# Order of gathers and scatters in the expert phase, and the length of four tanhs in the opening, of a Mamba and mixture-of-experts kernel

## The reference

```python
xn = layernorm(x)
# first layer, in outline
dA = exp(soft_clamp(dt * A, -8, 8, 0.5))          # soft_clamp is a tanh
def step(h, (dA_t, dB_t, x_t, C_t, t)):
    h = h * dA_t + dB_t * x_t
    fac = min(20 / (norm(h) + 1e-8), 1)           # norm over all of one sequence's state
    h = where(t % 10 == 0, h * fac, h)
    return h, einsum('bdn,bn->bd', h, C_t) + D * x_t
x = x + (xn + scale * (y * silu(gate)) @ W_out.T)
# second layer
gate = softmax(layernorm(x) @ Wg); idx = argmax(gate)
loc = place of the token among those of its expert;  valid = loc < 256
h = relu(einsum('ecm,emf->ecf', dispatched, w1))   # 16 x 256 x 512
expert_out = einsum('ecf,efm->ecm', h, w2)
x = x + (layernorm(x) + expert_out[idx, loc] * (gate[idx] * valid))
```

## Time and profile before

| | us |
|---|---|
| median of 3 runs | 693.81 (693.71 to 693.98) |
| the profiled execution | 692.75 |
| its span, from the first to the last instruction | 690.9 |
| busy: PE | 611.2 (88%) |
| busy: POOL | 581.4 (84%) |
| busy: DVE | 556.6 (81%) |
| busy: ACT | 520.2 (75%) |

### The profile page before, as it was taken

One profiled execution on the slowest core, in us unless ns is written; L12 is line 12 of the kernel. 1 busy time (PEld: TensorE's weight loads), 2 busy tenths in 40 slices (PEclk: granted clock), 3 DMA queues, 4 the chain that ended last, 5 costly groups with the idle time before them and its releaser, 6 DMA issues.

```text
span 690.9 us, 12862 instructions
## 1 busy us (share of the span) xinstructions
PE 611.2 (88%) x4108; PEld 476.0 (69%) x4108; DVE 556.6 (81%) x893; ACT 520.2 (75%) x1012; POOL 581.4 (84%) x413
## 2 busy tenths in 40 slices
PE   8689999999899999989999998999989994599981
PEld 6347677767677677767768677867768783589971
DVE  5658999999999989989999999999989985813320
ACT  3699989999999999999999999999977622112220
POOL 5179999999999999999999999998979972177775
PEclk9989999999999999999999999999999998599996
DMA  4241433236145323724441353325134203446731
GB/s 102 82 153 62 158 111 131 63 118 207 59 150 156 121 68 105 219 72 142 115 148 51 136 176 116 120 73 162 62 121 158 96 1 92 133 144 201 228 106 32
DMA packets 60025, 82.08 MB, mean 119 GB/s; under 512 B 14845, under 2 KB 40738, under 8 KB 59958
## 3 DMA queue, kind: packets, MB, share of 16 engines
q1 hardware_dynamic: 56400, 74.79, 34.1%
q0 software_dynamic: 2608, 6.21, 3.0%
q10 hardware_dynamic: 950, 0.27, 0.2%
HBM read 69.75 MB, written 11.72 MB: 118 GB/s over the span
## 4 chain that ended last, share of the span: by engine, by line
POOL 59%; issue 20%; PE 12%; DVE 3%; DMA 2%; POOLq 1%; ACTq 0%; SPq 0%; ACT 0%; DVEq 0%
POOL h L852 30%; POOL h L866 19%; PE ps L603 3%; PE ps L590 3%; POOL u L839 3%; POOL fac L881 1%; POOL out_dram L399 1%; POOL lnp L813 1%; POOL rstd L888 1%; PE ps L1652 1%; PE ps L610 1%; POOL cq L876 1%; PE ps L570 1%; DMA b0b<-b_d 1%; PE ps L563 1%
## 5 line engine op out<-in xcount | busy, mean ns | idle before, releaser
L1376 DVE TENSOR_TENSOR_SCAN h<-ps,h 128x902 f32<-128x902 f32 x204 | 320.0, 1609 | 21.5 <-ACT ps L993 12.6
L852 POOL TENSOR_TENSOR h<-u,scr 128x1280 f32<-128x1280 f32 x104 | 283.5, 2742 | 2.4
L1768 PEld LDWEIGHTS ps<-h,ident 128*128 128x128 f32 x1632 | 224.7, 190 | 21.8 <-issue 17.3
L1768 PE MATMUL ps<-h,ident 128*128 128x160 f32 x1632 | 231.0, 300 | 1.1 <-issue 0.8
L1102 ACT ACTIVATE z<-dtb,asc 128x240 f32<-128x240 f32 (+3 forms) x432 | 201.5, 536 | 0.1
L993 ACT ACTIVATE ps<-z 128x820 f32<-128x820 f32 (+1 forms) x208 | 137.9, 688 | 21.7 <-DVE h L1376 18.0
L866 POOL TENSOR_TENSOR h<-h,scr 128x1280 f32<-128x1280 f32 (+1 forms) x52 | 138.1, 2656 | 0.7 <-DVE h L1392 0.7
L1427 DVE TENSOR_TENSOR h<-h,ps 128x640 f32<-128x640 f32 (+1 forms) x155 | 87.9, 578 | 0.5 <-issue 0.2
L1652 PE MATMUL ps<-xnT,wT 128*128 128x488 f32 x144 | 72.1, 612 | 0.0
L1003 ACT ACTIVATE sqb<-h 128x208 f32<-128x208 f32 x102 | 45.0, 442 | 26.3 <-DVE h L1376 23.5
L391 POOL DMA_INDIRECT z<-rows_d,gidx x32 | 32.8, 1026 | 32.5 <-DVE gidx L510 23.0
(11 more groups left out here) (203 smaller groups left out, 811.4 us busy)
## 6 DMA issues: line engine op xcount, KB each, us to landing
scr<-b_d SPq DMA_DIRECT2D x52, 640.0 KB, 4.7
scr<-c_d SPq DMA_DIRECT2D x52, 320.0 KB, 4.3
z<-in_L_ffn_w_dram SPq DMA_DIRECT2D x32, 256.0 KB, 3.6
xx_d<-xx SPq DMA_DIRECT2D x8, 256.0 KB, 2.0
xxr<-xx_d SPq DMA_DIRECT2D x8, 256.0 KB, 2.6
rows_d<-h2b SPq DMA_DIRECT2D x16, 120.0 KB, 2.1
rows_d<-xxr SPq DMA_DIRECT2D x16, 120.0 KB, 2.2
out_dram<-xxr SPq DMA_DIRECT2D x16, 120.0 KB, 2.6
```

Of the source, the lines that this page charges most:

```text
L852: pool.tensor_tensor(hr[:, hf * RH:(hf + 1) * RH, 1:SLOT].rearrange("p (n b) t -> p n b t", b=B), us.unsqueeze(1).to_broadcast([P, NST, B, ...
L1376: dve.tensor_tensor_scan(hs, region(G)[:, 0:(r1 - r0) * SLOT], hs, 0.0, ALU.mult, ALU.add).then_inc(gscan, 1)
L1768: pe.matmul(ps[:, YB, 0:H * BS], ident[:], hr[:, :, n * B:(n + 1) * B, 0:SEG], start=(n == 0), stop=False)
```

## The change

Two edits, in POOL's and in ACT's program.

```diff
+        FIRST = 4
...
             pool.wait_ge(idx_ready, 2)
-            for e in range(E):
+            for e in range(AHEAD - 2):
                 pool.wait_ge(fin_made, e + 1)
                 scatter(e)
-                if e + AHEAD < E:
-                    gather(e + AHEAD)
+            for e in range(AHEAD, E):
+                gather(e)
+            for e in range(AHEAD - 2, E):
+                pool.wait_ge(fin_made, e + 1)
+                scatter(e)
...
             def second_half(v, k0, k1):
-                for k in (list(range(NST)) if v == 0 else HALVES)[k0:k1]:
+                for k in (range(max(k0, FIRST), k1) if v == 0 else HALVES[k0:k1]):
                     row_tanh(v, k, HALF * SEG, WIN)
...
-            opening_rows(0, 11, HALF * SEG)
+            opening_rows(0, FIRST, WIN)
+            opening_rows(FIRST, 11, HALF * SEG)
             decay(0)
```

## The result

| | before | changed |
|---|---|---|
| median, us | 693.71 (692.82 to 693.98, 5 runs) | 699.57 (696.78 to 700.38, 5 runs) |
| the profiled execution, us | 692.75 | 700.38 |
| its span, us | 690.9 | 698.6 |
| mean clock granted to PE | 0.965 | 0.955 |

The ratio is 1.0076, with a 95% interval of 1.006 to 1.0093: 0.8% slower, 5.3 us (the medians are 5.9 apart). In a second set of runs it was 1.0082 (1.0069 to 1.0095). The forecast had the sign and +3.5 us, and its range ended at 698.7. The changed kernel spreads over 3.6 us from run to run in this set, the kernel before over 1.2 (over 2.9 and 4.8 in later sets of 23 and 29 runs).

A forecast was written before the change was run, and what follows sets the result against it. The prediction took POOL to bound the expert phase and ACT the opening's first segment. Its terms -0.27 - 0.78 + 3.2 + 1.3 made +3.5 us, a median of 697.3 us, with a range of 695.3 to 698.7.

The forecast's parts named there:

- The bound: POOL ends the expert phase, its 64 indirect DMAs without further gaps; a wait inserted on POOL is paid in full.
- Part 1, the opening: Whole tanhs on ACT: 0.79 us delay swallowed by POOL's 1.10 us idle time, everything behind moves by -0.27 us.
- the second rival: The opening's delay stays: +0.79 us in place of -0.27, 698.4 us; chance 0.12.
- Part 2, fewer changes of kind: Expert phase on POOL: seven fewer changes between gathers and scatters at 0.11 us each, -0.78 us.
- Part 3, the waits on POOL: Expert phase: scatters in a row wait for DVE's results, which come 3.73 us apart; +3.2 us.
- The price of a release: On POOL, a blocked queue pays 0.87 us from release to DMA start; with only 0.30 us, waits would be 2.6.
- Part 4, the stall and its clock: PE idles over 8 us before the ninth expert, then runs at half clock, delaying the last scatters: +1.3 us.
- The first rival: PE doesn't hold up the end; only the waits on POOL are paid: +2.2 us, 696.0 us; chance 0.20.
- The sum: Whole kernel: -0.27 - 0.78 + 3.2 + 1.3 = +3.5 us, median 697.3 us.
- The upper end of the range: 698.7 us, from a long clock return (+0.7) and half of the opening's delay.

The follow-up runs named there:

- eight_scatters: Opening as before; against the changed order on POOL, four experts' scatters between the gathers in place of six: ratio 1.0032 to the kernel before, +2.2 us.
- open_again: The kernel before with only the four whole tanhs of the opening, old order on POOL, second set of runs: ratio 1.0029 to before, +2.0 us.
- both_again: The changed kernel with both edits, run and profiled a second time: 699.25 us, ratio 1.0082 to the kernel before.
- one_by_one: The kernel before with one scatter and one gather by turns in place of two and two: ratio 1.0004, DMA stretch 83.07 us.
- before_again: The unchanged kernel before, run and profiled a second time: 693.96 us, ratio 1.001.
- tail_only: The kernel before with only the new order of gathers and scatters on POOL, opening as before: ratio 1.0062, +4.3 us.

## Why the prediction was wrong, point by point

**The bound** was read rightly. POOL ends the expert phase, and a wait inserted there is paid in full; eight_scatters gave that to 0.03 us.

**Part 1, the opening, had the wrong sign.** ACT's +0.79 and -1.58 us are in the rows (first root +0.61 to +0.83, the scan behind ACT no longer waits while the clock is up). The step that failed is "if the norm comes 0.3 us earlier than before, and its scans have 0.65". The norm needs more than its scans: DVE's queue has the product by the gate of the segment before ahead of it, which waits for PE's sum over the states; PE's queue has that same sum ahead of the norm's; and PE's chain starts with an input that DVE makes right behind the first norm, which is 0.8 us late. In the profile of before this chain and the scans ended together (the scans at 61.73, the product by the gate at 61.65 without a wait), so no idle time pointed at it:

```profile
61.65 0.32 DVE L1361 TENSOR_TENSOR yg<-ps,sgn 128x160 f32<-128x160 f32 x1
```

The second root measured +0.7 and +0.8 us (open_again and both_again, where the clock stayed up) in place of -0.27. This was the second rival, with a chance of 0.12, and what I put against it ("ACT passes its old place at 57.71 earlier") was true and beside the point.

**Part 2, fewer changes of kind, was right in size**: 0.8 us, and the changed kernel's stretch less its waits is 82.08 us, 0.86 below 82.94 (0.9 with all eight gone). As a price of one change that can be multiplied it was wrong: one_by_one has twice the changes and 0.13 us more.

**Part 3, the waits on POOL, is the term that was mis-sized**: +3.2 us, and 4.8 to 5.6 were measured. The step is "the results of the fourth to sixth expert end at 630.41, 634.14 and 637.87". Those were the times of one execution, in which the clock didn't fall during the product of the gates. In ten of the thirteen profiles it falls, and the second to sixth result come 1.6 to 2.5 us later behind the first gather (the second result of both_again 23.2 us behind, of changed and before_again 24.0, in place of 21.55). The kernel before hides this: POOL came to the second scatter 5.0 us after its result (627.94 against 622.95), and to each further one later still. I had looked for how much PE is ahead in the trace, and not for whether that trace's PE was typical. The price of a release was nearly right: 0.79 to 0.80 us from the end of the result to the start of the scatter (628.03 to 628.82), where I had 0.87 and not 0.30.

**Part 4, the stall and its clock, was right in its picture and four to six times too large in its price.** PE stood still for 8.21 us, the gather came 2.84 us after its issue (647.68 to 650.52; I had 2.88), the clock fell to 0.50 at 645.8. But it was back 5.5 us after PE resumed, where I had taken 7.2, which makes 2.7 us lost in place of 3.6, and POOL's own lateness by part 3 left the last results more room: 0.35 us of waiting in the changed kernel, 0.21 in tail_only, in place of 1.3. The first rival, in which PE doesn't hold up the end at all, was closer on this point than the forecast. (The earlier return that I gave as 5.7 us, to 41.6, is 5.6 by its window, to 41.44; the sum doesn't hang on it.)

The Trainium skill, "TensorE: Matmul & The Clock Gate", section "HAM oscillation — how this bites in real kernels", agrees with the trace in that PE resumes from a long wait for a DMA at the lower clock (0.50 in the windows 646 to 656) and loses half of that time. As a warning for the whole kernel it didn't decide anything here, since POOL and not PE was behind the end. The estimate from "DMA: Bandwidth & Descriptors", section "Anatomy of one DMA", 2.3 us for such a gather, stays 0.5 below the 2.84 measured.

**The sum**, with measured terms: +0.8 for the opening, -0.8 for the mixing, +5.2 for the waits, +0.3 for the late one: +5.5 us, against 5.3 (4.2 to 6.5) and 5.7 (4.8 to 6.6) measured. The upper end of the range, by the terms named for it (+0.7 and half of the opening's 1.06), is 698.5 and not 698.7. The 7.7 us between the spans of the two profiled executions have another 1.7 us in them from the clock behind the opening (13.06 us from root to root in place of 11.37), which also falls without either edit. About 0.3 us are left ahead of the first gather; a fall of the clock near 516 us lasted 6.8 us in place of 3.4 there, but that it cost this isn't shown.

What stays open: whether the longer tanhs make the fall of the clock behind the opening more likely. Five of nine profiles against three of five tell nothing, and the mean clocks of the runs tell little (0.9591 over the twelve of open_again, 0.9601 over the 29 of the kernel before beside them). open_again's +2.0 us is more than the 0.8 that its rows show, and this could be one reason; it wasn't tried. Open too is why the clock falls in the product of the gates in some executions and not in others.

## What to carry to other kernels

Before two queues are put closer together, ask how far the one behind was ahead in executions other than the profiled one: a lead of 5 us had hidden a clock that comes and goes, and giving it up made the end wait for it. A chain that ends together with the one that you follow shows no idle time and is yet the next bound; look at every operation that the queue puts ahead of the one you count on. And put work that waits for nothing (here all gathers) ahead of work that waits, as long as there is room for its results: it made the DMA stretch 0.9 us shorter here, though the time only by an amount that the runs can't tell from nothing.

## What the runs showed of the hardware

- PE's clock fell to 0.50 while PE's rows were full: 32 bf16 products of 96 columns in 5.5 us, 2.00 of 2.00 us busy in the windows 612 to 616. In ten of thirteen profiles it fell there, for 3.4 or 6.8 us, in three it didn't. Here the busy share didn't tell whether the clock would hold.
- The place where the clock changes shifts from execution to execution: the first fall of each profile, in the same idle time of PE (6.4 to 7.0 us long, from about 27 us on), came between 29.1 and 32.1 us.
- An indirect DMA of 128 rows costs POOL 1.30 (gather) or 1.29 us (scatter) in rows of one kind and 1.32 to 1.33 in the mean where both are mixed, whether by pairs or singly. From the end of a result to the start of the scatter that waits for it are 0.80 us.
